# Loading eight input blocks as four pairs, and the small parameter load behind the weights, in a two-pass scan with GroupNorm

## The reference

```python
def step(prev, x_i):
    y = jnp.einsum('oc,nch->noh', Wc, prev) + conv_b[None, :, None]
    y = jnp.where(y >= 0, y, prelu_a * y)
    cur = y + x_i
    return (cur, cur)
x = jnp.moveaxis(feature, 3, 0)                 # feature = _gn(x): mean and variance over
_, fwd_rest = jax.lax.scan(step, x[0], x[1:])   # 16 channels, H and W, for each image
fl = jnp.concatenate([x[0:1], fwd_rest], axis=0)
_, bwd_rest = jax.lax.scan(step, fl[-1], fl[:-1], reverse=True)
```

## Time and profile before

| | us |
|---|---|
| median of 3 runs | 377.96 (377.9 to 378.09) |
| the profiled execution, its own time | 378.02 |
| its span, first to last instruction | 376.5 |
| PE busy | 351.9 |
| the prelude, up to the first matmul of line 338 | 40.25 |

### The profile page before, as it was taken

One profiled execution on the slowest core, in us unless ns is written; L12 is line 12 of the kernel. 1 busy time (PEld: TensorE's weight loads), 2 busy tenths in 40 slices (PEclk: granted clock), 3 DMA queues, 4 the chain that ended last, 5 costly groups with the idle time before them and its releaser, 6 DMA issues.

```text
span 376.5 us, 10084 instructions
## 1 busy us (share of the span) xinstructions
PE 351.9 (93%) x3096; PEld 350.3 (93%) x3096; DVE 287.2 (76%) x927; ACT 228.1 (61%) x803; POOL 19.3 (5%) x30
## 2 busy tenths in 40 slices
PE   0269999999999999999999999999999999999996
PEld 0169999999999999999999999999999999999995
DVE  2678997887888878655656778778778787787786
ACT  3765556566565565665665655656656656556564
POOL 2177000000000000000000000000000000000000
PEclk9999999999999999999999999999999999999999
DMA  7998000000000000000000112212212212122122
GB/s 304 423 412 311 2 0 0 1 0 0 1 0 0 1 0 0 0 0 0 0 0 0 57 67 74 84 56 84 84 56 84 78 62 84 64 76 84 56 111 84
DMA packets 10808, 26.30 MB, mean 70 GB/s; under 512 B 1328, under 2 KB 1584, under 8 KB 10800
## 3 DMA queue, kind: packets, MB, share of 16 engines
q1 hardware_dynamic: 10656, 26.22, 18.0%
q10 hardware_dynamic: 144, 0.00, 0.0%
HBM read 13.63 MB, written 12.58 MB: 70 GB/s over the span
## 4 chain that ended last, share of the span: by engine, by line
PE 90%; DMA 6%; SPq 2%; DVE 1%; ACT 0%; issue 0%; ACTq 0%
PE psum L338 88%; DMA xin<-in_x 6%; SPq L228 2%; PE psum L293 1%; PE psum L303 1%; DVE state L436 0%; DVE state L492 0%; DVE state L487 0%; ACT state L359 0%; PE psum L267 0%; ACT state L362 0%; PE psum L286 0%; ACT above L406 0%; PE psum L262 0%; PE psum L284 0%
## 5 line engine op out<-in xcount | busy, mean ns | idle before, releaser
L338 PE MATMUL psum<-state,w_t 128*128 (+1 forms) x2976 | 332.7, 275 | 0.0
L338 PEld LDWEIGHTS psum<-state,w_t 128*128 128x128 f32 x2976 | 332.5, 192 | 0.1
L406 ACT ACTIVATE above<-psum,params 128x128 f32<-128x128 f32 x376 | 140.1, 373 | 132.3 <-PE psum L338 128.8
L487 DVE TENSOR_TENSOR state<-above,state 128x128 f32 (+1 forms) x376 | 108.4, 288 | 66.7 <-ACT above L406 65.4
L408 ACT ACTIVATE below<-psum,negative 128x128 f32<-128x128 f32 x376 | 140.4, 374 | 0.0
L492 DVE SCALAR_TENSOR_TENSOR state<-below,negative,state 128x128 f32 (+1 forms) x376 | 123.6, 349 | 7.1 <-DVE state L487 0.2
L534 DVE TENSOR_TENSOR state<-state,xin (+1 forms) x45 | 30.8, 684 | 0.0
L418 DVE BATCH_NORM_STATS2 bstat<-xin 128x6 f32<-128x512 f32 x33 | 21.1, 678 | 12.3 <-DMA xin<-in_x 12.3
L436 DVE TENSOR_SCALAR state<-xin,mean,rstd 128x320 f32<-128x320 f32 (+3 forms) x73 | 28.6, 439 | 0.0
L254 PE MATMUL psum<-chan,centre 128*128 128x64 f32 (+1 forms) x8 | 2.0, 348 | 17.9 <-DVE chan L432 17.9
L254 PEld LDWEIGHTS psum<-chan,centre 128*128 128x128 f32 x8 | 1.6, 255 | 18.1 <-issue 13.5
(11 more groups left out here) (38 smaller groups left out, 26.2 us busy)
## 6 DMA issues: line engine op xcount, KB each, us to landing
out_y<-state SPq DMA_DIRECT2D x47, 256.0 KB, 2.0
xin<-in_x SPq DMA_DIRECT2D x13, 768.0 KB, 12.7
xin<-in_x SPq DMA_DIRECT2D x7, 256.0 KB, 17.7
w_t<-in_w SPq DMA_DIRECT2D x4, 256.0 KB, 10.3
xin<-in_x SPq DMA_DIRECT2D x1, 512.0 KB, 19.6
out_y<-state SPq DMA_DIRECT2D x1, 192.0 KB, 1.9
out_y<-state SPq DMA_DIRECT2D x1, 64.0 KB, 1.6
params<-in_par ACTq DMA_DIRECT2D x1, 2.5 KB, 4.9
```

The costliest lines, as they stand in the source:

```text
L338: mm = nc.tensor.matmul(psum[:, 4 * par + o, 0:COLS], w_t[:, k, o * P:(o + 1) * P], xs[k], start=k == 0, stop=k == 3)
L406: nc.scalar.activation(above[:, par, o, :], z, ACT.Relu, bias=params[:, o:o + 1], scale=1.0).then_inc(above_done, 1)
L487: nc.vector.tensor_tensor(sts[o], above[:, par, o, :], sts[o], ALU.add).then_inc(part_done, 1)
```

## The change

Three edits. The host lays x out as (tile, partition, image, W, H), so that two neighbouring images of one tile are 12 KB without a gap in a partition. Blocks (2, 3), (4, 5), (6, 7) and (8, 9) are each one load of 1536 KB with one semaphore, which both blocks share. The load of `params` leaves ACT's queue, where it was the first thing issued, for SP's queue behind the weights, and ACT's negation of it moves from behind block 0's statistics to just ahead of the scan.

```diff
+PAIRS = {2: 3, 4: 5, 6: 7, 8: 9}
...
-    KT, N, _, W, H = x.shape
+    KT, _, N, W, H = x.shape
...
         x_loaded = [[sem(f"x_loaded{b}_{i}") for i in range(len(pieces(b)))] for b in range(NBLK)]
+        for first, second in PAIRS.items():
+            x_loaded[second] = x_loaded[first]
...
-            for b in range(NBLK):
+            for b in (b for b in range(NBLK) if b not in PAIRS.values()):
+                n1 = (PAIRS[b] if b in PAIRS else b) % N + 1
                 w0 = 0
                 for i, size in enumerate(pieces(b)):
-                    sp.dma_start(xin[:, b // N, b % N, w0:w0 + size, :],
-                                 x[b // N, b % N, :, w0:w0 + size, :]).then_inc(x_loaded[b][i], 16)
+                    sp.dma_start(xin[:, b // N, b % N:n1, w0:w0 + size, :],
+                                 x[b // N, :, b % N:n1, w0:w0 + size, :]).then_inc(x_loaded[b][i], 16)
                     w0 += size
             for k in range(KT):
                 sp.dma_start(w_t[:, k, :], w[k * P:(k + 1) * P, :]).then_inc(w_loaded[k], 16)
+            sp.dma_start(params[:, :], par[:, :]).then_inc(params_loaded, 16)
...
-            act.dma_start(params[:, :], par[:, :]).then_inc(params_loaded, 16)
             act.wait_ge(counts_set, 4)
...
             unit_stats(0)
-            act.wait_ge(params_loaded, 16)
-            nc.scalar.mul(negative[:, :], params[:, :], -1.0).then_inc(negated, 1)
             unit_stats(1)
...
             group_values(3)
+            act.wait_ge(params_loaded, 16)
+            nc.scalar.mul(negative[:, :], params[:, :], -1.0).then_inc(negated, 1)
             act.wait_ge(negated, 1)
...
-        "in_x": x.reshape(N, KT, P, H, W).transpose(1, 0, 2, 4, 3),
+        "in_x": x.reshape(N, KT, P, H, W).transpose(1, 2, 0, 4, 3),
```

## The result

| | before | changed |
|---|---|---|
| median of 14 runs, us | 377.89 | 378.54 |
| lowest and highest | 377.77, 378.21 | 377.80, 379.30 |
| profiled execution, its own time | 378.02 | 378.53 |
| its span | 376.5 | 376.7 |
| first matmul of the scan (line 338, now 344) | 40.25 | 40.60 |

The ratio of the times is 1.0018, with a 95% interval of 1.0011 to 1.0026: slower, by 0.4 to 1.0 us. What the median hides is the spread, the distance from the lowest run to the highest: 0.4 us before, 1.5 us now.

A forecast was written before the change was run, and what follows sets the result against it. The start was taken as bound by x's queue, then ACT and PE's gapless string into PE's scan. The sum, 0.65 (D late) - 0.17 (a PE wait gone) = +0.48 us, gave 378.44 us, range 377.6 to 379.2.

The forecast's parts named there:

- D: Start of batch 2's squares on ACT, which moves PE's string and the scan; forecast 30.5 against 29.85, late by 0.65 us.
- part 3's cases: Four cases for when TensorE's clock rises around PE's keep_up(9, 0); D was taken as 30.5 from them.
- the third case: Clock rises at 28.9 as before; PE's keep-up ends at 29.69 and D = 30.06.
- the second's: Clock rises 5.5 us after the variances start, at 30.36; PE's keep-up ends at 30.42 and D = 30.79.
- What the loads gain: Part 1, x's queue: longer rows and the moved parameter load bring blocks 8 and 9 from 22.52 to 22.14, 0.38 us.
- the straight line: Fit of DMA row time, 37.5 ns a KB and a fixed 10 ns a row: a 12 KB row takes 460 ns.
- that is its price: Moving the parameter load off the start of x's queue was counted as gaining 0.08 us of every engine.
- the new layout of x reads no better: Lower bound in part 1: the loads' gain is nothing if the new layout reads no better.
- From D to the scan: Part 4: PE's string to line 284 has no gap; one wait, at line 286, goes and gives back 0.17 us.
- The parameters: Part 5: negation ahead of the scan costs nothing if the load lands by 39.2; landing late had chance 0.03.
- A fixed cost in series: Rival on the loads: fixed cost paid one after another, 0.08 us each, 0.3 us for four; more had chance 0.01.
- Slower than 0.2%: Rival that the prelude slips by more: D at 30.79 or later, from +0.76 us on; chance 0.31.

The follow-up runs named there:

- e1: The changed kernel with blocks 8 and 9 loaded apart again, the other three pairs kept; median 377.75 us.
- e2: The changed kernel with (8, 9) as the only pair; median 378.59 us.
- e7: The changed kernel with keep_up(9, 0) of 5 turns for 6, so 10 matmuls for 12; median 378.06 us.
- the four profiles: The profiled executions in which ACT waited for PE; own time is the start of batch 2's squares plus 347.9 us, within 0.11.
- e11: The kernel before, on the old layout without pairs, with the late parameter load on SP's queue and the late negation; median 378.01 us.
- e10: The changed kernel without pairs and with the parameters loaded first from ACT again, so the new layout only; median 378.56 us.
- e3: The changed kernel without any pair: new layout and late parameters alone; median 378.31 us.
- e12: The kernel before, old layout, no pairs, with parameters issued by ACT behind block 14 and the negation just ahead of the scan; median 377.73 us.
- e4: The changed kernel with batch 1's squares and values ahead of block 8 on ACT; median 379.27 us.
- e9: e4 with keep_up(9, 0) of 8 turns for 6; median 377.83 us.

## Why the prediction was right, point by point

**The mechanism** was as forecast, each step in its place: the pair lands late, ACT's block 8 at 22.30 (forecast 22.18), batch 1's squares at 24.75 (24.63), block 12 at 28.38 (28.34), the keep-up from 25.46 (25.33), its end between the cases, D at 30.57 (30.5), and a spread from the clock's rise. This is shown by e1 and e2 (which pair), by e7 (that the keep-up is what is waited for), and by the four profiles (that the time follows D). Of part 3's cases none met the rise of the clock: it came at 29.4, between the third case's 28.9 and the second's 30.36, after some 4.5 us of PE's work and not 5.5.

**What the loads gain.** The 12 KB row takes 460 ns in the trace, as the straight line gave. The landing of (8, 9) is at 22.24 and not 22.14. The step that was mis-sized is that on the parameters, "0.08 us of every engine; that is its price". Its packets take no more than that, yet moving it lets x start 0.34 to 0.54 us sooner (before and e11, e10 and e3). And "the new layout of x reads no better" allowed for no gain but not for a cost: it costs 0.34 to 0.54 at the start. That the two cancelled was luck, since the sum had 0.08 for the one and nothing for the other; what is left is the pairs' 0.28, where 0.3 was forecast.

**From D to the scan.** "PE's string ... has no gap" was wrong in small: it took 10.40 us from D to the scan before and 10.03 now, so 0.37 is given back and not 0.17. The spacing of 0.28 between lines 281 and 284, which I took for back to back, held a wait for `off`, which DVE wrote from 35.29 to 35.50 in the kernel before:

```profile
35.29 0.21 DVE L459 TENSOR_SCALAR off<-chan,shift 128x1 f32<-128x1 f32 x1
```

Without it the spacing is 0.17, and line 286 (now 292) follows after 0.22, where it was 0.45. So 0.11 and 0.23 come back there; 0.09 more comes back ahead of line 281, and 0.06 is lost again between the last sums and the scan. PE in the changed kernel:

```profile
35.91 0.33 PE L287 MATMUL psum<-chan,same_group 128*128 128x64 f32 x2
36.08 0.39 PE L290 MATMUL psum<-off,same_group 128*128 128x64 f32 x2
36.30 0.39 PE L292 MATMUL psum<-off,same_group 128*128 128x64 f32 x2
```

**The end.** I counted nothing behind the scan. From the last store's issue to the end it is 3.91 us now and 3.75 before, +0.16; why stays open. So the sum against the profile is 0.72 (D) - 0.37 + 0.16 = +0.51, where 0.65 - 0.17 = +0.48 was forecast: the total was closer than its terms, which is luck too. By the medians the change is +0.65.

**The parameters** landed in time, ACT's negation at 36.76 after 0.57 us of waiting, 2.4 us before the next need:

```profile
36.76 0.21 ACT L403 ACTIVATE negative<-params 128x5 f32<-128x5 f32 x1 [0.57 <-DMA params<-in_par]
```

**The rivals.** A fixed cost in series of more than the 0.08 us a load that the sum has is excluded: a pair lands 3.68 us behind the one ahead (DVE's waits end at 18.56 and 22.24), and two single blocks took 3.76. Slower than 0.2% happened in 5 of the 14 runs, 379.11 to 379.30, and not in the median. That their clock rose late is argued from the four profiles above, of which e2's (379.53, the keep-up at the lower level nearly to its end) is that long; none of the five was profiled.

## What to carry to other kernels

Merging two loads gives both tiles the landing time of the second, so look at what stands in program order behind the consumer of the first: here it was not that consumer that paid but a small step queued behind it, and a loop of idle matmuls behind that on another engine. Pair so that the tile held back is one whose consumer has nothing urgent behind it. A keep-up loop is a piece of work with a start and an end: it wants its size chosen again whenever its start moves. Here a wider spread of the runs went with it both times, when it ended too late and when it ended too early, so a spread that grows is a reason to look at it.

## What the runs showed of the hardware

- A load of 144 tiny packets, issued at the same time from another queue, put off the landing of the first large loads: block 1's statistics started 0.18 us (e12), 0.34 (e11) and 0.54 (e3 against e10) sooner without it, though its packets took 0.08 us of each engine. The scatter of that start within one configuration is 0.33.
- With 6 KB rows 24 KB apart for consecutive partitions in place of 6 KB apart, block 1 landed 0.34 us (e3 against e11) to 0.54 us (e10 against before) later, with medians 0.40 and 0.59 apart, and the later blocks came at the same cadence of 1.88 us.
- The granted clock fell to 0.50 while PE was busy, behind a stretch in which it had worked 1.73 of 3.30 us, in the profiled execution of e4; 7 of its 12 runs have about that execution's time, 5 are some 1.5 us shorter. In e9, where PE worked 2.21 of the same 3.30 us, it did not fall.
- 26 and not 25 loads on SP went with 0.36 us more between the last store and the end (e3 and e11 against before).
